# The first mixture's way out, moved into the third norm's loop over chunks

## What is computed

```python
h = tok(x)                                   # splice 3 frames, project to 128
h = h + recurrence(layernorm(h))             # complex linear recurrence
h = h + mixture_1(layernorm(h))              # 16 experts, top 2
h = h + sparse_attention(layernorm(h))       # 8 heads, 25 chosen queries
h = h + mixture_2(layernorm(h))              # 64 experts, top 42

# mixture_1, last steps: y_mean is a table, one row of 128 for each expert
y_mean = einsum('ef,edf->ed', h_mean, w2)
out = einsum('tk,tkd->td', routing_w, y_mean[top_idx])
```

## Time and profile before

| | us |
|---|---|
| median of 3 runs | 2138.89 (2136.77 to 2153.66) |
| the profiled execution, its own time | 2138.86 |
| span of the profiled execution, first to last instruction | 2137.1 |
| mean granted clock of TensorE over the span | 0.923 |
| way out of the first mixture, from the copy of `ym` to the last add's start | 475.84 to 492.40 |
| third norm, from its first load of weights to its last step on DVE | 493.40 to 518.23 |

### The profile page before, as it was taken

The page is one execution under the profiler, slowest core; times in us unless marked ns, Lnnn a source line. Parts: engine busy times, 40 slices in busy tenths (PEclk is TensorE's granted clock), DMA queues, the critical chain, the costliest instruction groups (busy, mean ns, idle before and its releaser), DMA issues.

```text
span 2137.1 us, 50727 instructions
## 1 busy us (share of the span) xinstructions
PE 1885.2 (88%) x17146; PEld 1354.1 (63%) x17146; DVE 1676.4 (78%) x4764; ACT 1388.1 (65%) x2070; POOL 1349.4 (63%) x1026
## 2 busy tenths in 40 slices
PE   7889300888998987799999999999999999999998
PEld 5556200455657875567777777777777777777776
DVE  4775730853567767879999999999999999999998
ACT  3112350742443544488888888888888888888886
POOL 2100177005970003288989999988898989888887
PEclk9999655997998996599999999999999999999999
DMA  3612181612320002000000100000200000000000
GB/s 90 179 40 99 56 302 59 121 39 65 98 79 1 1 1 82 1 1 2 0 0 0 76 6 1 0 0 1 81 2 0 0 0 2 2 10 10 10 10 18
DMA packets 73497, 82.63 MB, mean 39 GB/s; under 512 B 38564, under 2 KB 56516, under 8 KB 71684
## 3 DMA queue, kind: packets, MB, share of 16 engines
q1 hardware_dynamic: 70660, 75.19, 11.6%
q0 software_dynamic: 2688, 5.44, 0.8%
HBM read 42.97 MB, written 29.20 MB: 34 GB/s over the span
## 4 chain that ended last, share of the span: by engine, by line
PE 56%; DVE 3%; issue 1%; POOL 0%; ACT 0%; ACTq 0%; DVEq 0%; POOLq 0%
PE bank L2339 29%; PE bank L2322 27%; DVE m_work L2212 1%; DVE m_best L2209 0%; DVE m_work L2203 0%; DVE m_ut L792 0%; PE bank L2291 0%; DVE m_best L2202 0%; DVE m_ex L2214 0%; ACT m_h L2153 0%; DVE h L2250 0%; POOL m_h L2098 0%; DVE m_red L2215 0%; DVE m_row L2195 0%; PE bank L784 0%
## 5 line engine op out<-in xcount | busy, mean ns | idle before, releaser
L2339 PEld LDWEIGHTS bank<-weights,m_h 128*128 128x128 f16 x10752 | 639.1, 98 | 190.0 <-DVE hc L2241 91.6
L2098 POOL TENSOR_TENSOR m_h<-m_hidden,m_h 128x896 f16<-128x896 f32 x384 | 725.2, 1888 | 31.9
L2241 DVE SCALAR_TENSOR_TENSOR hc<-bank,m_shares,hc 128x128 f32<-128x128 f32 x2688 | 727.0, 342 | 4.1 <-PE bank L2339 4.1
L2339 PE MATMUL bank<-weights,m_h 128*128 128x128 f16 x10752 | 724.4, 219 | 2.4 <-POOL m_h L2098 2.4
L2150 ACT ACTIVATE m_hidden<-bank,m_b 128x896 f32<-128x896 f32 x384 | 386.7, 1007 | 184.2 <-PE bank L2322 184.1
L2228 DVE TENSOR_TENSOR m_h<-bank,m_h 128x896 f16<-128x896 f32 x384 | 419.2, 1092 | 108.8 <-ACT m_h L2153 108.8
L2096 POOL TENSOR_SCALAR m_h<-m_hidden 128x896 f16<-128x896 f32 x384 | 359.8, 937 | 111.5 <-ACT m_hidden L2150 83.0
L2322 PE MATMUL bank<-m_u_first,weights 128*128 128x448 f16 (+1 forms) x1536 | 417.8, 354 | 6.9 <-DVE h L2250 5.5
L2322 PE MATMUL bank<-m_u_second,weights 128*128 128x448 f16 (+1 forms) x1536 | 417.4, 353 | 0.0
L2147 ACT ACTIVATE bank<-bank,m_b 128x896 f32<-128x896 f32 x384 | 377.2, 982 | 0.4 <-PE bank L2322 0.4
L2153 ACT ACTIVATE m_h<-bank 128x896 f16<-128x896 f32 x384 | 348.7, 908 | 0.0
(11 more groups left out here) (328 smaller groups left out, 2143.7 us busy)
## 6 DMA issues: line engine op xcount, KB each, us to landing
weights<-expert_factors SPq DMA_DIRECT2D x12, 1024.0 KB, 8.6
expert_slots<-lru_zeros SPq DMA_DIRECT2D x1, 8256.0 KB, 31.9
lw_raw<-e_w_dram SPq DMA_DIRECT2D x16, 512.0 KB, 4.8
expert_factors<-lw_made SPq DMA_DIRECT2D x16, 512.0 KB, 4.6
ew_raw<-e_w_dram SPq DMA_DIRECT2D x16, 512.0 KB, 4.4
lru_wst<-w_dram SPq DMA_DIRECT2D x16, 256.0 KB, 2.7
weights<-w_dram SPq DMA_DIRECT2D x1, 4096.0 KB, 12.7
expert_factors<-ew_made SPq DMA_DIRECT2D x8, 512.0 KB, 3.1
```

Source lines behind the costliest of these rows:

```text
L2098: g.tensor_tensor(h1[:, x, 1], hidden[:, x], h1[:, x, 0], ALU.subtract).then_inc(second_of[1], 1)
L2241: last = v.scalar_tensor_tensor(acc[:, m * TW:(m + 1) * TW], y[q][:, (n - start) * TW:(n - start + 1) * TW], shares[:, m, e:e + 1], acc[:, ...
L2339: last = t.matmul(y[q][:, (n - start) * TW:(n - start + 1) * TW], factors[:, m, n * TW:(n + 1) * TW], k.weights[:, grp % 2, 2 + m, at], st ...
```

## The change

`ym` becomes a buffer of the whole kernel. `first_mixture` ends with the copy of the table into it: the 14 products, the 14 adds and their semaphores are gone. `norm_statistics` gets a parameter `outputs`, given for `n3` alone. With it PE has a further product for each of the norm's 16 chunks of 332 (`added`), into banks 5 and 6 in turn, and DVE a further add to `k.h` for each (`add`). `added` of chunk c waits for the add of chunk c - 2 (its bank), `means` of chunk c waits for the add of chunk c, and DVE centres a chunk after it has added three chunks further on. PE's order is then added 0, 1, 2, means 0, added 3, means 1, means 2, and for every chunk c: added c + 4, means c + 3, variances of c. DVE's is add 0, 1, 2, and for every chunk c: add c + 3, centre c. The other three norms issue what they did before. The diff:

```diff
--- before.py
+++ after.py
@@ -364,13 +364,15 @@
 DEEP, AHEAD = 4, 3
 
 
-def norm_statistics(nc, k, name, table, pieces=None, width=CH, tile=HALF, count=NC):
+def norm_statistics(nc, k, name, table, pieces=None, width=CH, tile=HALF, count=NC, outputs=None):
 
 
     tiles = count * (width // tile)
     with ExitStack() as ctx:
         sq = ctx.enter_context(nc.sbuf_tensor(f"{name}_sq", [128, DEEP, width], F32))
         st = ctx.enter_context(nc.sbuf_tensor(f"{name}_st", [tile, 4, tiles], F32))
+        out_ready = k.semaphore(f"{name}_out_ready")
+        h_added = k.semaphore(f"{name}_out_added")
         mean = k.semaphore(f"{name}_mean")
         centred = k.semaphore(f"{name}_centred")
         squared = k.semaphore(f"{name}_squared")
@@ -405,13 +407,26 @@
         def _(pe):
             pe.sem_inc(var, DEEP)
 
+
+
+            def added(c, j):
+
+                if not isinstance(c, int) or c >= 2:
+                    pe.wait_ge(h_added, c - 1)
+                nc.tensor.matmul(k.bank[:, DEEP + 1 + j % 2, 0:width], outputs, k.hc[0:E0, span(c)], start=True,
+                                 stop=True).then_inc(out_ready, 1)
+
             def means(c, j):
 
+                if outputs is not None:
+                    pe.wait_ge(h_added, c + 1)
                 pe.wait_ge(centred, c + 1)
                 nc.tensor.matmul(k.bank[:, j, 0:width], k.mean_w[:], k.h[:, span(c)], start=True, stop=True).then_inc(mean, 1)
 
             def work(c, j):
 
+                if outputs is not None and (not isinstance(c, int) or c + DEEP < count):
+                    added(c + DEEP, j)
                 if not isinstance(c, int) or c + AHEAD < count:
                     means(c + AHEAD, (j + AHEAD) % DEEP)
                 pe.wait_ge(squared, c + 1)
@@ -420,7 +435,12 @@
                                             sq[:, j, q * tile:(q + 1) * tile], k.mean_w[:, 0:1], start=True, stop=True)
                 last.then_inc(var, 1)
 
+            if outputs is not None:
+                for c in range(2):
+                    added(c, c)
             for c in range(AHEAD):
+                if outputs is not None and c + 2 < DEEP:
+                    added(c + 2, c + 2)
                 means(c, c)
             chunks(pe, work)
 
@@ -433,7 +453,22 @@
                 nc.vector.tensor_tensor(k.hc[:, span(c)], k.h[:, span(c)], k.bank[:, j, 0:width],
                                         ALU.subtract).then_inc(centred, 1)
 
-            chunks(dve, centre, 0)
+            def add(c, j):
+                dve.wait_ge(out_ready, c + 1)
+                nc.vector.tensor_tensor(k.h[:, span(c)], k.h[:, span(c)], k.bank[:, DEEP + 1 + j % 2, 0:width],
+                                        ALU.add).then_inc(h_added, 1)
+
+            def add_and_centre(c, j):
+                if not isinstance(c, int) or c + AHEAD < count:
+                    add(c + AHEAD, (j + AHEAD) % DEEP)
+                centre(c, j)
+
+            if outputs is None:
+                chunks(dve, centre, 0)
+            else:
+                for c in range(AHEAD):
+                    add(c, c)
+                chunks(dve, add_and_centre)
             dve.wait_ge(var, count + DEEP)
             nc.vector.tensor_scalar(st[:, 0], v, EPS, None, ALU.add).then_inc(step, 1)
             dve.wait_ge(root, 1)
@@ -841,8 +876,8 @@
         part = sb("part", [128, NST, FC])
         part_t = sb("part_t", [NST, FC * 128])
         hsum = sb("hsum", [128, FC, E0 * E0])
-        ym = sb("ym", [E0, 128])
         xt = sb("xt", [128, RING, 2, ST], F16)
+        ym = k.ym
         rt = k.hc[0:E0, :]
 
         gate_in = sem("gate_in")
@@ -870,9 +905,6 @@
         by_expert = sem("expert_sums")
         gathered = sem("expert_gathered")
         y_ready = sem("y_ready")
-        y_kept = sem("y_kept")
-        out = sem("out_ready")
-        added = sem("out_added")
         block = ctx.enter_context(nc.Block())
         w0 = k.weights[:, 0].rearrange("p a b -> p (a b)")
         w0_parts = w0[:, 0:E0 * FF0], w0[:, E0 * FF0:]
@@ -1045,10 +1077,7 @@
             dve.wait_ge(by_expert, 1)
             v.tensor_copy(hsum[:, :, 0:E0 * E0:E0 + 1], k.bank[:, 1, 0:FC * E0].rearrange("p (f e) -> p f e", f=FC)).then_inc(gathered, 1)
             dve.wait_ge(y_ready, 1)
-            v.tensor_copy(ym[:], k.bank[0:E0, 7, 0:128]).then_inc(y_kept, 1)
-            for c in range(NCW):
-                dve.wait_ge(out, c + 1)
-                v.tensor_tensor(k.h[:, span(c)], k.h[:, span(c)], k.bank[:, c % 4, 0:CW], ALU.add).then_inc(added, 1)
+            v.tensor_copy(ym[:], k.bank[0:E0, 7, 0:128])
 
         @block.tensor
         def _(pe):
@@ -1105,11 +1134,6 @@
                     last = t.matmul(k.bank[0:E0, 7, 0:128], hsum[:, f, x * E0:(x + 1) * E0], w2[:, x, f, :],
                                     start=(x == 0 and f == 0), stop=(x == E0 - 1 and f == FC - 1))
             last.then_inc(y_ready, 1)
-            pe.wait_ge(y_kept, 1)
-            for c in range(NCW):
-                if c >= 4:
-                    pe.wait_ge(added, c - 3)
-                t.matmul(k.bank[:, c % 4, 0:CW], ym[:], rt[:, span(c)], start=True, stop=True).then_inc(out, 1)
 
 
 class Choice:
@@ -2416,6 +2440,7 @@
         k.mean_w = sb("mean_w", [128, 128])
         k.ones = sb("ones", [128, 128])
         k.cells = sb("cells", [1, 8])
+        k.ym = sb("ym", [E0, 128])
         k.hm = sb("hm", [128, NH])
         k.sel = sb("sel", [128, E0 + 1, 128], F16)
         k.weights = sb("weights", [128, 2, 4, GE * HC * 128], F16)
@@ -2439,7 +2464,7 @@
         first_mixture(nc, k)
         with ExitStack() as inner:
             k.expert_weights = ExpertWeights(nc, k, inner)
-            norm_statistics(nc, k, "n3", 5, PIECES_N3)
+            norm_statistics(nc, k, "n3", 5, PIECES_N3, outputs=k.ym[:])
             sparse_attention(nc, k)
             norm_statistics(nc, k, "n4", 6, None, CW, TW, NCW)
         second_mixture(nc, k, out)
```

## The result

The changed kernel took 2155.17 us (median of 14 executions, 2151.37 to 2159.0), the kernel before 2137.6 beside it (14, 2133.8 to 2153.66). The ratio of the executions is 1.0067 with a 95% interval of 1.0048 to 1.0085: 14.3 us slower, with 10 and 18 as ends. The two medians are 17.6 apart, inside that interval; the kernel before spreads more widely, with 3 of its 14 executions at 2149 us or above. The forecast was 2152 us, 12.8 slower, with 2145 to 2158 as its own range. The profiled executions are 2151.37 and 2138.86 us, 12.5 apart.

What follows compares the result with a forecast made beforehand. PE's own work was taken to bound the place. All low clock costs 16.1 us; less two high chunks (2 x 1.67), 12.8 us on 2138.9 gives 2152 us; own range 2145 to 2158, with rivals 2127 to 2162.

Steps and rivals of the forecast that it cites:

- The clock: Norm's loop: TensorE's granted clock falls in the first chunks and stays low to the norm's end; all low is 16.1 us later.
- the first rival: Norm's loop: the clock holds high, 16 x 1.67 us cheaper than low, 10.1 us faster than before, 2128.8 us; chance 0.18.
- The second, half of the norm: Norm's loop: clock holds for eight chunks, 2.7 us more than before, 2141.6 us; chance 0.09.
- Two chunks at high: Norm's start: two chunks run at high clock before the fall, each worth 1.67 us, leaving 12.8 us more than before.
- A chunk at low clock: Norm's loop: added product 1.107, means 1.107 and variances 1.20 make 3.41 us a chunk, 54.6 us for 16.
- the variances' 1.20 us: Norm's loop: a chunk's variances on PE at low clock, taken between at least 1.04 and 1.27 us.
- the product in 1.107: Norm's loop: a 332-column product, two PE instructions of 0.553 us at low clock, its height not mattering for length.
- The tail: Norm's end: 3.4 us from DVE's step behind the last variance to the next stage, taken from the old kernel's 3.35.
- The waits at nothing: Norm's loop: PE, DVE and ACT waits covered by chunks ahead, costing nothing at low clock, about 0.5 us at high.
- the third rival: Norm's loop: clock high but waits uncovered, an add of 0.56 us each chunk, 1.1 us faster, 2137.8 us; chance 0.05.
- POOL hidden: Beside the norm: expert-weight loads and POOL's splitting, 24.2 us from 476.4 to 500.6, end before the norm does.
- The chances: Whole kernel, about 1% or 21 us distinguishable: faster 0.01, same 0.92, slower 0.07; the forecast itself 0.68.

## Why the prediction was right, and where its terms were off

The forecast of the stage, from the copy's end to attention's first transfer, was 0.44 + (54.6 - 3.34) + 3.4 = 55.1 us; it is 56.4. The cause, the level of the clock and the time were right. That the stage is off by only 1.3 us is in part luck: 16 chunks at the low level were 6.0 us dearer than forecast (60.6 for 54.6), and 3.8 of high clock and 1.0 of the tail came back.

- **The clock** (right). It fell in the new loop's first chunks and stayed low to the norm's end, because of the height of the added product. With 16 partitions the first rival, that the clock holds, is out; with 96 or 128 it is what the kernel does: 2130.8 and 2127.5 us, where I had worked out 2128.8 for it. The second, half of the norm, is near what 64 partitions do (2142.6 against 2141.6).
- **Two chunks at high** (mis-sized). The clock was 1.00 for 8.1 us of PE's work, 475.0 to 483.1. 16 chunks at 3.79 would be 60.6 us; PE's part took 528.5 - 475.0 = 53.5, so 7.1 were given back, at 3.79 - 2.03 = 1.76 a chunk four chunks' worth, not two. That is this execution, the fastest of 14; their median is 3.8 us above it, which would be two chunks' worth (an estimate, 3.8/1.76).
- **A chunk at low clock** (mis-sized: 3.41, measured 3.79; at high 1.74, measured 2.03). I had named the variances' 1.20 us as the uncertain term, and a chunk off 3.4 as a sign of it; by 488.69 - 487.56 they took 1.13. What failed is the product in 1.107: from the added product's start to the means' it is 486.30 - 484.90 = 1.40, and from there to the variances' 487.56 - 486.30 = 1.26. 0.29 + 0.15 - 0.07 is the 0.38 but for rounding. I had read a product's length where its own kind follows it, with only 0.31 us of "issue" ahead of each load, and had not asked what stands between two products of different heights. The full-height load there doesn't run beside the product on 16 partitions. The kernel with one extra product shows both at the low level, a full-height product behind the 16 partitions (L430) and one behind its own kind (L424):

```profile
505.07 1.48 PE L430 MATMUL bank<-ones,mean_w 128*128 128x332 f32 x2
506.34 1.31 PE L424 MATMUL bank<-h,mean_w 128*128 x2
507.45 0.77 PE L435 MATMUL bank<-mean_w,n_sq 128*83 128x1 f32 x5
```

- **The tail** (mis-sized: 3.4, measured 530.89 - 528.53 = 2.4). I carried the old tail over. In it, as in the kernel without products, one small operation of DVE ended only when POOL's splitting was done (at 515.30 + 2.12 = 517.42); two rows of the kernel before, in order of time:

```profile
515.70 0.55 DVE L440 RECIPROCAL n_st<-n_st 83x64 f32<-83x64 f32 x1 [0.32 <-ACT n_st L462]
516.28 1.21 DVE L443 TENSOR_TENSOR n_st<-n_st 83x64 f32<-83x64 f32 x1
```

The reciprocal, which reads a single operand, ran beside the same POOL operation in its usual 0.55 us. In the new kernel POOL was done at 498.5, and the second operation (L478 above) takes 0.22 us. That gave back 1.0 us that I hadn't counted.
- Together: 60.6 - 7.1 = 53.5 against 51.3, with 0.1 more at the start and 1.0 less at the end, is 55.1 + 2.3 - 1.0 = 56.4.
- **The waits at nothing** (right). DVE idles for PE, not PE for DVE, and without the adds it is no faster; the third rival falls. One sign was wrong: only the adds wait for PE (33.3 us idle), the centring hardly does (2.0).
- **POOL hidden** (right here; it becomes the bound when the loop gets to 19 us).
- **The chances** (right): no case reached 1%; the interval of the ratio ends at 0.85%.

What stays open: what in PE's work exactly the clock follows. Height weighs, and full-height products offset it, but one extra a chunk lost the level after 18 us and two brought it back and kept it, and 64 partitions did either. Nor do these runs say when it falls: two loops that begin with the same products on 16 partitions kept it for 8.1 us (the changed kernel) and 3.7 us (without the adds). Also not tried: whether the gap goes away if the added product stands elsewhere in the chunk.

The Trainium skill, TensorE: Matmul & The Clock Gate, section "Why this matters for your kernels", looks at idle gaps between bursts. By it the loop would have kept its clock; 45.00 of 45.00 us busy at 0.50 says that the absence of gaps is not enough.

## What to carry to other kernels

A matmul whose contraction fills few of the 128 partitions takes as long as a full one (two instructions of 332 columns at the high level: 0.82 us on 16 partitions, 0.80 on 128), but it can take the clock from everything around it, so before it is moved into a loop that runs at the high level, read the granted clock in the place where it stands now. If the clock is low there though PE never idles, pad the operand with zero rows to the full height first: here that was worth 7 us in the old place and 28 in the new one (24 of them seen in the stage), and it turned a move that lost 14 us into one that wins 3. And read what stands next to what: the cost of an instruction behind its own kind isn't its cost behind another.

## What the runs showed of the hardware that I hadn't expected

- A full-height weight load doesn't overlap a product on 16, 32 or 64 partitions (0.46 us of "issue" idle ahead of it at clock 1.00, 0.91 at 0.50); behind 96 or 128 partitions it does (the load at 482.01 in the row of 128 partitions, under a product of 481.64 to 482.44).
- The clock can come back in the middle of a loop with PE never idle: 0.57 at 475 to 480 and 1.00 from 485 on, with two extra full-height products a chunk.
- A DVE operation with two SBUF operands, started beside a POOL operation of the same kind, ended within 0.1 us of it: 2.00 and 1.21 us for 0.22. One with a single SBUF operand wasn't held (0.55 us either way). The Trainium skill says so in its table of specifications (GPSIMD Engine Reference, section "1. Specifications"): the SBUF interfaces are shared with VectorE, with contention for instructions of two SBUF inputs. The traces agree. Where such an operation is in the chain at a stage's end, it can cost up to the rest of the other engine's operation: 1.8 us here at most (2.00 for 0.22).
